# Gate and up of the last two FFN groups as seven half-block products in place of eight, with attention in short pieces between them

## The reference

```python
x = x + attn(layernorm(x))         # gated delta recurrence over the tokens, K=64, V=128
x = x + ffn(layernorm(x))
# ffn, d=512, h=1408, q(w) = clip(round(w / mean|w|), -1, 1), so each weight is -1, 0 or 1
hidden = sigmoid(x @ q(w1).T) * (x @ q(w2).T)
y = hidden @ q(w3).T
```

## Time and profile before

| | |
|---|---|
| timed runs | 328.49 us median of 3 (328.21 to 328.55) |
| span of the profiled execution | 327.07 us; the page gives it no other time, so the median stands 1.42 us above its span |
| granted TensorE clock, mean | 1.000 |
| busy share: TensorE, VectorE, ScalarE, GpSimd | 98%, 64%, 44%, 33% |
| group 3's gate and up, and its downs, on TensorE | 37.99 us and 19.06 us |

### The profile page before, as it was taken

The page is one execution under the profiler, slowest core; times in us unless marked ns, Lnnn a source line. Parts: engine busy times, 40 slices in busy tenths (PEclk is TensorE's granted clock), DMA queues, the critical chain, the costliest instruction groups (busy, mean ns, idle before and its releaser), DMA issues.

```text
span 327.1 us, 5876 instructions
## 1 busy us (share of the span) xinstructions
PE 319.8 (98%) x2152; PEld 176.1 (54%) x2152; DVE 210.1 (64%) x474; ACT 142.4 (44%) x281; POOL 107.4 (33%) x339
## 2 busy tenths in 40 slices
PE   7999999999999999999999999999999999999996
PEld 5888779874445444445454444454544444444445
DVE  6789899899998767366688543666886312433311
ACT  3687896789855571323143260231431102232200
POOL 7298325599913016980030136500201100000000
PEclk9999999999999999999999999999999999999999
DMA  6999900647841625300003051000030720000011
GB/s 180 382 388 395 360 4 0 104 91 133 125 85 32 114 49 81 113 0 2 0 2 64 2 129 61 7 2 0 2 64 0 93 102 1 0 2 0 0 66 64
DMA packets 45805, 26.99 MB, mean 83 GB/s; under 512 B 37584, under 2 KB 38352, under 8 KB 45776
## 3 DMA queue, kind: packets, MB, share of 16 engines
q1 hardware_dynamic: 45456, 26.62, 31.0%
q10 hardware_dynamic: 320, 0.00, 0.0%
HBM read 13.89 MB, written 4.19 MB: 55 GB/s over the span
## 4 chain that ended last, share of the span: by engine, by line
PE 78%; DVE 10%; DMA 3%; SPq 3%; ACT 2%; issue 2%; DVEq 0%; ACTq 0%
PE ffn L1199 40%; PE ffn L1217 23%; PE lev L1120 4%; DMA x_sb<-in_L_attn_x_dram 3%; PE ffn L1044 3%; DVE w_nat L841 2%; DVE X L854 2%; SPq L282 2%; PE lev L1077 2%; PE pd L1054 2%; PE oc L1104 1%; DVE abs_part L821 1%; DVE w_nat L848 1%; DVE xnT L989 1%; DVE sc L881 1%
## 5 line engine op out<-in xcount | busy, mean ns | idle before, releaser
L1199 PE MATMUL ffn<-w_nat,w12T 128*128 128x512 f16 x704 | 155.4, 379 | 0.6 <-DVE xnT L989 0.6
L1199 PEld LDWEIGHTS ffn<-w_nat,w12T 128*128 128x128 f16 x704 | 67.8, 98 | 83.0 <-issue 3.7
L1217 PE MATMUL ffn<-w3T,w_nat 128*128 128x512 f16 (+1 forms) x374 | 76.7, 366 | 0.0
L718 ACT ACTIVATE xnT<-ffn 128x512 f32<-128x512 f32 x44 | 26.1, 593 | 97.5 <-PE ffn L1199 97.5
L989 DVE SCALAR_TENSOR_TENSOR xnT<-ffn,xnT 128x512 f32<-128x512 f32 x44 | 30.2, 687 | 52.3 <-PE ffn L1199 51.9
L1217 PEld LDWEIGHTS ffn<-w3T,w_nat 128*128 128x128 f16 x374 | 36.6, 98 | 40.7 <-ACT w_nat L724 1.0
L402 POOL TENSOR_TENSOR ve<-mv,rconst 128x2 f32<-128x2 f32 x12 | 2.5, 210 | 118.1 <-DVE mv L758 118.1
L1005 DVE SCALAR_TENSOR_TENSOR x_sb<-ffn,x_sb 128x512 f32<-128x512 f32 (+1 forms) x17 | 11.2, 659 | 42.8 <-PE ffn L1217 42.8
L994 DVE TENSOR_TENSOR w_nat<-xnT,w_nat 128x512 f16<-128x512 f32 x44 | 32.2, 732 | 0.4
L724 ACT ACTIVATE w_nat<-xnT 128x512 f16<-128x512 f32 x44 | 27.4, 623 | 8.4 <-DVE xnT L989 8.3
L881 DVE COPY_PREDICATED sc<-mask,lev 128x128 f32<-128x128 uint32 x56 | 18.9, 338 | 2.9 <-PE oc L1091 1.3
(11 more groups left out here) (142 smaller groups left out, 368.2 us busy)
## 6 DMA issues: line engine op xcount, KB each, us to landing
x_sb<-in_L_attn_x_dram SPq DMA_DIRECT2D x16, 256.0 KB, 8.4
out_dram<-x_sb SPq DMA_DIRECT2D x15, 256.0 KB, 2.0
w_nat<-in_L_ffn_w_dram SPq DMA_DIRECT2D x2, 1536.0 KB, 12.2
w_nat<-in_L_ffn_w_dram SPq DMA_DIRECT2D x2, 1408.0 KB, 14.7
w_nat<-in_L_ffn_w_dram SPq DMA_DIRECT2D x2, 1280.0 KB, 12.9
wv<-in_L_attn_Wv_dram SPq DMA_DIRECT2D x1, 256.0 KB, 5.8
wo<-in_L_attn_Wo_dram SPq DMA_DIRECT2D x1, 256.0 KB, 13.5
out_dram<-x_sb SPq DMA_DIRECT2D x2, 128.0 KB, 1.7
```

The costliest lines, as they stand in the source:

```text
L718: nc.scalar.activation(sig[:, u % 2, :], bank[2 * u % 3][:, :], ACT.Sigmoid, scale=1.0 / XS).then_inc(sig_ready, 1)
L1199: done = nc.tensor.matmul(bank[n % 3][:, :], w12T[:, a * DT + t, u * P:(u + 1) * P], xT[:, g, part, t, :], start=t == 0 and part == 0, sto ...
L1217: done = nc.tensor.matmul(bank[(2 * HT + m + h) % 3][:, cols], hid[:, part, j, m * P:(m + 1) * P], w3T[:, j, cols], start=part == 0 and j ...
```

## The change

For groups 2 and 3 the 2x2 block product (gate and up rows by two halves of the contraction, times the two batches) is made in Winograd's form of Strassen's scheme. It needs seven products of half blocks in place of eight: per unit seven times 4 matmuls (2 tiles, 2 halves) of 256 columns (HP). It also needs sums.

- Sums of weights (T1 to T4, exact in float16, 2 x 1408 numbers in each partition) are made once on VectorE in group 1, at units 3:2, 2:3, 4:4, 1:11 (`T_AT`: unit and T).
- Sums of x: four of 256 numbers for each chunk 4 to 7, on GpSimd (on VectorE for chunk 7). They are split into high and low halves like the parts of x that stay (`xhiN`, three blocks; `xhiS`, the four sums). `xlo` on GpSimd becomes four operations of 256. The transposes of a chunk are two, of 1536 and of 2048 columns, in place of two of 1024.
- Sums of products are made in part in PSUM. ScalarE copies P1 to the second bank (`seed`), on which P2 and P6 go on adding, keeps copies U2 and U3, and takes the sigmoid in two halves. VectorE adds P5's and P3's banks to the kept copies (`up_b`, `up_a`). GpSimd multiplies sigmoid with up in two halves (`hidden_b`, `hidden_a`).
- A scale of 512 in place of 2048 is used for these tokens. The projection weights' storage and other dead buffers are used again.
- The first product of a group (P1) is put in front of the last four down matmuls of the group before.
- Attention of chunk 6 starts earlier: chain0 and chain1 before the adds of down products 2 and 3 of group 1, levels behind down product 3. Chunk 6 needs `fetch` for that, which follows chunk 5's xlo on GpSimd. The stages on VectorE are cut into pieces. Levels, o and wo of chunks 6 and 7 stand behind units -1 and 5, 1 and 8, 2 and 9.
- Some matmuls of the first down product come between the last products of unit 10.

The core of the diff:

```diff
+        DVE_NEXT_FAST = DVE_AFTER | {"xlo": (8, 13)}
+        ACT_NEXT_FAST = {"gt": (2, 7), "oT": (4, 9), "xhiN": (7, 12), "xhiS": (8, 13)}
+        SP_NEXT_FAST = {"turn": (9, 13)}
+
+        PE_FAST = {"levels": (-1, 5), "o": (1, 8), "wo": (2, 9)}
+        DVE_FAST = {"chain0": (-2, None), "chain1": (-1, None),
+                    "chainA": (None, 2.5), "chainB": (None, 3), "chainC": (None, 3.5), "chainD": (None, 4),
+                    "chainE": (None, 4.5), "masks0": (0, 6.5), "masks1": (0, 7), "masks2": (0, 7.5),
+                    "masks3": (0, 8), "state": (2, None), "resid0": (5, 10.5), "resid1": (6, 11),
+                    "xlo": (DOWN, DOWN + 2), "xloS": (None, DOWN + 2), "norm2a": (8.5, DOWN), "norm2b": (9, DOWN),
+                    "apply": (10, DOWN + 1), "sums": (None, DOWN + 1)}
+        ACT_FAST = {"gt": (0, None), "oT": (2, 9), "xhiN": (HT, HT + 2), "xhiS": (HT + 1, HT + 2)}
+        POOL_FAST = {"fetch": (-1, 0), "sums0": (10, None), "sums1": (11, None), "xlo": (HT + 1, None),
+                     "norm2": (9, HT + 1)}
+        SP_FAST = {"turn": (HT + 1, HT + 2)}
...
+        T_AT = {2: (3,), 3: (2,), 4: (4,), HT: (1,)}
...
+            def sums0(c):
+
+                pool.wait_ge(xn2_ready, B * c + 2)
+                pool.wait_ge(xhi_ready, B * c)
+                pool.wait_ge(xlo0_ready, c)
+                pool.wait_ge(tile_T, 2 * C)
+                nc.gpsimd.tensor_tensor(xsum[:, 2, :], A11(0), A11(1), ALU.subtract)
+                link(nc.gpsimd.tensor_tensor(xsum[:, 0, :], A11(1), A12(1), ALU.add))
+
+            def sums1(c):
+
+                link(nc.gpsimd.tensor_tensor(xsum[:, 1, :], xsum[:, 0, :], A11(0), ALU.subtract))
+                nc.gpsimd.tensor_tensor(xsum[:, 3, :], A12(0), xsum[:, 1, :], ALU.subtract).then_inc(sums_ready, 1)
...
+                for c in (2 * g + 2, 2 * g + 3):
+                    norm2(c)
+                    if is_fast(c):
+                        sums0(c)
+                        sums1(c)
+                    xlo(c)
+                if g + 2 < G and g + 1 in FAST:
+                    fetch(2 * g + 4)
...
+            for g in FAST:
+                for k in range(HT + 2):
+                    if k > 1:
+                        hidden_a(g, k - 2)
+                    for s, c in POOL_AT.get((g, k), ()):
+                        attn(s, c)
+                    if 1 <= k <= HT:
+                        hidden_b(g, k - 1)
...
+                for k in range(HT + 1):
+                    if k > 0:
+                        keep_u3(g, k - 1)
+                    if k < HT:
+                        seed(g, k)
+                    if k > 1:
+                        hidden_hi(g, k - 2)
+                    for s, c in ACT_AT.get((g, k), ()):
+                        attn(s, c)
+                    if k < HT:
+                        keep_u2(g, k)
+                    if k > 0:
+                        sigmoid_b(g, k - 1)
+                    if k < HT:
+                        sigmoid_a(g, k)
...
+            def weight_sum(n):
+
+                if n == 3:
+                    done = nc.vector.tensor_tensor(T3, up_w[1], up_w[0], ALU.subtract)
+                if n == 2:
+                    done = nc.vector.tensor_tensor(T2, T3, gate_w[0], ALU.add)
+                if n == 4:
+                    done = nc.vector.tensor_tensor(T4, gate_w[1], T2, ALU.subtract)
+                if n == 1:
+                    done = nc.vector.tensor_tensor(T1, up_w[0], gate_w[0], ALU.subtract)
+                done.then_inc(T_ready, 1)
...
+            def product(out, weights, u, tokens, first):
+
+                for t in range(2):
+                    for part in range(2):
+                        done = nc.tensor.matmul(out[:, 0:HP], weights[:, t, u * P:(u + 1) * P], tokens[:, part, t, :],
+                                                start=first and t == 0 and part == 0, stop=t == 1 and part == 1, skip_group_check=not first)
+                return done
...
+                for k in range(HT):
+                    if k > 0:
+                        product1(g, k)
+                        product5(g, k - 1)
+                        product4(g, k - 1)
+                    product6(g, k)
+                    product2(g, k)
+                    if k > 0:
+                        product3(g, k - 1)
+                    product7(g, k)
+                    for s, c in PE_AT.get((g, k), ()):
+                        attn(s, c)
```

More of the change, by code:

```diff
@@ L361, in _ @@
                             turn_w3(j)
[L362 to L365, removed]
+                    for s, c in SP_AT.get((g, u), ()):
+                        turn_x(c)
                     if u >= HT:
@@ L500, in _ @@
             for u in range(UNITS):
[L501 to L503 removed]
+                for s, c in POOL_AT.get((0, u), ()):
+                    if (s, c) != ("fetch", 2):
+                        attn(s, c)
                 if u == 3:
@@ L510, in _ @@
             gates(4)
-            for g in range(1, G - 1):
+            for g in range(1, FAST[0]):
                 fetch(2 * g + 2)
@@ L739, in _ @@
             for g in range(G):
-                group(g)
+                if g in FAST:
+                    fast_group(g)
+                else:
+                    group(g)
         @block.vector
@@ L878, in attn @@
                     scores = lev[:, :].rearrange("p (b n) -> p b n", b=B)
-                    for l in range(NL):
+                    for l in {"masks": range(NL), "masks0": (0, 1), "masks1": (2, 3), "masks2": (4, 5), "masks3": (6,)}[s]:
                         n, h = P // 2 ** (l + 1), 2 ** l
@@ L1206, in group @@
                         bank_free(g, 2 * HT + m)
[L1207 to L1215, removed]
-                                            pe.wait_ge(w3_in[j % QS], 16 * (j // QS + 1))
-                                    done = nc.tensor.matmul(bank[(2 * HT + m + h) % 3][:, cols],
-                                                            hid[:, part, j, m * P:(m + 1) * P], w3T[:, j, cols],
-                                                            start=part == 0 and j == 0,
-                                                            stop=part == 1 and j == HT - 1)
-                            done.then_inc(down_done, 1)
@@ L1222, in group @@
-                    if g < G - 1:
-                        for s, k in stages(PE_AFTER, u):
-                            attn(s, 2 * g + 2 + k)
+                        for n in range(2 * HT):
+                            if m == 0:
+                                pe.wait_ge((hi_ready, lo_ready)[n // HT], g * HT + n % HT + 1)
+                                if g == 0 and n < HT:
+                                    pe.wait_ge(w3_in[n % QS], 16 * (n // QS + 1))
+                            if m == DT - 1 and n == 2 * HT - 4 and g + 1 in FAST:
+                                pe.wait_ge(xT_in, 64 * g + 128)
+                                product1(g + 1, 0)
+                            down(g, m, n, PARTS_IN_TURN)
@@ L1225, in group, with down @@
+                    for s, c in PE_AT.get((g, u), ()):
+                        attn(s, c)
                     if g == 0 and u == 0:
                         spread(1)
+            PARTS_IN_TURN = [(part, j) for part in range(2) for j in range(HT)]
+            LATE_LAST = ([(part, j) for part in range(2) for j in range(HT - 3)]
+                         + [(part, j) for j in range(HT - 3, HT) for part in range(2)])
+            def down(g, m, n, order):
+                part, j = order[n]
+                done = nc.tensor.matmul(down_bank(g, m)[:, :], hid_at(g, part, j, m), w3T[:, j, :], start=n == 0,
+                                        stop=n == 2 * HT - 1)
+                if n == 2 * HT - 1:
+                    done.then_inc(down_done, 1)
@@ new lines, in down_last @@
+            def down_last(g, m):
+                for h in range(2):
+                    cols = slice(h * D // 2, (h + 1) * D // 2)
+                    for n, (part, j) in enumerate(PARTS_IN_TURN):
+                        done = nc.tensor.matmul(down_bank(g, m + h)[:, cols], hid_at(g, part, j, m), w3T[:, j, cols],
+                                                start=n == 0, stop=n == 2 * HT - 1)
+                    done.then_inc(down_done, 1)
+            def product(out, weights, u, tokens, first):
[4 more added lines that the diff above has]
+                return done
```

397 lines of the change are left out of this document (351 added, 46 removed).

## The result

The changed kernel takes 331.42 us (median of 8 runs, 329.30 to 332.44), the kernel before 328.51 (8 runs). The ratio is 1.0073, interval 1.0057 to 1.0089: slower by 0.7%. The forecast was 326.3 us and faster, the range 322.5 to 330.4.

The account below looks back on a forecast made before the run. TensorE, busy 98% of the span, was taken as the bound. The terms -8.8 + 4.8 + 0.2 + 0.7 + 0.9 gave -2.2 us, 328.5 to 326.3 us; range 322.5 to 330.4 us, to hold 8 in 10.

Parts of the forecast that it names:

- The saving: Groups 2 and 3: a unit takes 3.055 us in place of 3.454, over 22 units -8.8 us.
- Does the loop keep pace: Units of groups 2 and 3: the other engines keep up with the seven products except for small waits, +0.2 us.
- The first seam: Group 1 to 2: levels(6) waits for chain(6), behind fetch(6) on GpSimd's queue, until about 207.4 us, +4.8 us.
- The weight sums: VectorE in group 1: four sums of 2816 f16 elements at 1.6 us each, upper end 3.1; T1 priced in the seam.
- The rival at one element a step: Weight sums on VectorE take 3.1 us each, delaying group 1 and the first seam: 329.6 us, chance 0.12.
- The table load: ScalarE, first unit of group 2: the load falls between U2(2,0) and the sigmoid, +0.7 us, or 0 if elsewhere.
- The second seam: Group 2 to 3: P1(3,0) waits for the transposed x of chunk 7, +0.9 us, between 0 and 1.5.
- No fall of the clock: TensorE's clock stays up in the seam; the rival, a fall to 1.2 GHz, gave 329.3 us, chance 0.10.
- The chances: Whole kernel: faster 0.65, same 0.09, slower 0.26; the forecast itself had 0.50.
- the full gain: Rival: the first seam is hidden, needing fetch(6) done early; 321.5 us, chance 0.13.

Follow-up runs that it names:

- Experiments 1 and 9: 1: the changed kernel with fetch(6) ahead of norm2(5) on GpSimd, 327.57 us, ratio 0.9966; 9: the run e10.
- experiment 2: The changed kernel with matmuls on a constant filling TensorE's three idle stretches at the seams, no wait removed: 329.79 us, ratio 1.0028.
- e3: Experiment 3: the changed kernel with resid1(6) moved from VectorE's unit 6 to unit 5: 331.63 us, ratio 1.0080.
- e8: The changed kernel with norm2(7) moved ahead of xlo(6), nothing else: 330.33 us, ratio 1.0036.
- e10: e9 with fetch(6) put back behind xlo(5): 330.49 us, ratio 1.0055.
- e9: e7 with the sigmoid's table load in unit 13, behind xhiS(5), in place of unit 12: 322.03 us, ratio 0.9799.
- e4: The changed kernel with fetch(6) ahead of norm2(5), and P1 of groups 2 and 3 behind the last four downs: 325.58 us, ratio 0.9903.
- e7: e6 with norm2(7) moved ahead of xlo(6): 323.98 us, ratio 0.9870.
- e5: e4 with the sigmoid's table load put behind exps(7) in group 1: 327.18 us, ratio 0.9945.
- e6: e5 with resid1(6) moved from VectorE's unit 6 to unit 5: 325.67 us, ratio 0.9915.

## Why the prediction was wrong, by its steps

Two things failed. The waits that the change puts into TensorE's queue were priced nearly 3 us too low in all, which is enough to turn "faster" into "slower" at full clock (329.3 against 328.5 us). And the clock fell behind them, which the sum had at nothing; this takes the median out of the range.

- *The saving, -8.8 us.* Right. A unit takes 3.055 us in the changed kernel, as worked out, and TensorE's busy time fell by 8.4. Group 3 alone was to be 4.4 us shorter: from its P1 at 271.01 to the end of the last downs at 324.94 it is 53.1 us without the four downs of group 2 in it, against 57.05 before, 4.0 us.
- *Does the loop keep pace, +0.2.* The steady units do, without a wait. In unit 0 of each group P7 comes 0.2 us late, behind U2 (0.05 forecast). But one wait was missed, a term that stood at nothing: levels(7), behind unit 5 on TensorE, needs resid1(6), which stands in VectorE's unit 6. It costs 0.8 us as listed, 0.92 by the pace of 109.1 ns a matmul (the last four matmuls ahead of it start at 228.67, levels(7) at 230.03). The prediction checked the new products' round trips and not each moved attention stage against the pieces it waits for.
- *The first seam, +4.8.* Right in cause, place and size: levels(6) at 207.26 us (forecast 207.4), waits of 1.7 and 3.0 us. The steps of the chain came within 0.5 us: T1 1.61 (1.6), xhiS 1.06 (1.05), xlo(5) 2.55 (2.75), fetch(6) to 201.63 (202.05). Experiments 1 and 9 show it: without it the time falls, with it alone it comes back.
- *The weight sums.* 1.62, 1.62, 1.62 and 1.61 us for T3, T2, T4 and T1, the lower end; TensorE waits nowhere in group 1 before the seam. The Trainium skill, "VectorE: DVE Perf Modes", section "The perf-mode tier table (the rule you actually need)", gives 2x for tensor_tensor on 16-bit operands: the trace agrees, 1.6 us for 2816 elements. The rival at one element a step (329.6 us) is out, although its number lies near the result. (Its own terms, 1.7 and 1.5 us, add up to 3.2 and not 3.3.)
- *The table load, +0.7.* Right: the load at 209.51 us between U2(2,0) and the sigmoid, a wait of 0.6. The sigmoid follows at 210.80, 0.01 us behind the load. The Trainium skill, "ScalarE: Activation LUTs", section "What ACT_TABLE_LOAD costs", adds a drain of 1.38 us; here too no row shows it.
- *The second seam, +0.9.* Mis-sized: 2.1 us. Counted from P5(2,10), which starts at 249.15 us, norm2(7) takes 2.1 us where the sum put 1.8 although its own row has 2.1; xlo(6) takes 2.92 (2.7); apply(7), the sums and the output add end 0.3 us later than their terms; the transpose of the sums is issued only when SP is done issuing the other one (266.14, 0.4 us late), and lands 4.82 us later (4.5). That is 1.4 us, of which 0.4 is hidden, since P1(3,0) too is due later.
- *The sum for a run at full clock.* 326.3 forecast, 329.3 measured, in the one run that has this clock: 3.0 us. By the pace of its matmuls, which is 0.16 us ahead of the ends from which the view counts a wait, the waits of the profiled run are 1.87 and 3.20 us in the first seam, 0.81 at the table load, 0.92 at levels(7) and 2.24 in the second seam. So the second seam is 1.3 us over its term, levels(7) 0.9, the first seam 0.3, P7 of the two units 0 gives 0.2 and the load 0.1: 2.8 of the 3.0. The 1.42 us kept for what lies around the span is 1.7 in this run.
- *No fall of the clock.* This step failed too, and it puts the median outside the range. The prediction had it as a rival with 0.10, at 329.3 us, and put it aside as "the waits here look short for it". (That the run without a fall also took 329.3 us is chance.) In seven of eight runs the clock fell. Together with the 3.0 us it gives 331.4, outside the range, because the range took each case alone and not two of them at once. That the idle time in the seams causes it is shown by experiment 2 (filled, clock 1.000 in all six runs), by e3, e8 and e10 (it falls at the end of the idle stretch), and by e9 (waits of 0.5 us at most, no fall in four runs). The cost was 2.05 us in e3, 1.9 in e8, 2.6 in e10. The Trainium skill, "TensorE: Matmul & The Clock Gate", section "What's actually happening", has TensorE's clock at 1.2 GHz after an idle time: the runs agree, and they show it also after stretches that are idle only in part, 1.47 us of work in 5 us in e3. Why it spares some runs of the same kernel isn't settled here; nothing in the program differs between them.
- *The chances.* Faster had 0.65, but the forecast and the full gain together have 0.63 at most.

So the change loses not through its arithmetic but through the order of the queues around it. The seven products are worth 2% once the waits are out.

## What to carry to other kernels

When an early stage is pulled forward on the bottleneck engine, follow every queue that its inputs pass, instruction by instruction, and check each wait that the moved stage already had. Here levels(7) went from unit 7 to unit 5 on TensorE, while half of the resid(6) it waits for went from unit 5 to unit 6 on VectorE. Price an idle stretch of TensorE at more than its length: a total of 4.7 us of waiting within 6.2 us cost 6.8, since the clock fell behind it (an estimate: the listed waits of the profiled run and the 2.1 us of e3). A cheap test for this is to fill the wait with matmuls that compute nothing and look whether the median moves.

## What the runs showed of the hardware

- Waits of 1.4 us can be enough. In e4 to e7 TensorE has one or two waits of 1.2 to 1.5 us at a seam, each with one of 0.5 us behind it, and 10 of the 19 runs show a mean clock of 0.995; with waits of 0.5 us alone (e9) none of four does. In the profiled runs of e4 to e7, all at 0.995, the clock falls right there: in e5, e6 and e7 in the first seam, in e4 in the second, behind 1.4 us of waiting for xT and 0.46 for the seed. I had thought a few microseconds of partial idleness safe. The windows of e4 (columns as in experiment 3):

```profile
266.00:268.00 2.00, 0.88 (x7) 0.56 (x8) 0.00 (x0) 0.37 (x1) 0.00 (x0) 0.99 0.53 201
268.00:270.00 2.00, 2.00 (x12) 1.37 (x10) 0.00 (x0) 0.77 (x2) 0.00 (x0) 0.50 0.00 0
```

- A fall comes in steps over the runs: means of 1.000, 0.995, 0.990 and 0.984. In the trace of e3 (0.990) the clock is low from 207.1 to 213.9 us. A lower mean is not always a longer time: in e10 the runs at 0.984 take 330.86 and 330.35 us, those at 0.990 take 330.58 and 330.41.
- A VectorE tensor_tensor on three float16 tensors takes 1.6 us for 2816 elements, 0.57 ns each. With float32 sources it takes 0.454 us for 256 elements and 0.73 for 512, about 1.1 ns for each element more.
- Four GpSimd operations of 256 columns in a row took 2.55 us in the first seam and 2.92 in the second (L606), in one and the same trace.
